# A down projection with seven block products in place of eight, and one load fewer of the packed half tile

## The chip, the cores and the metric

One core of one Trainium2 chip. The metric is the device time of one execution in microseconds: the kernel before takes 1940.79 us (median of 3 runs, 1940.75 to 1940.89). Besides, one execution was recorded by the hardware profiler. The engines are TensorE (PE; its weight loads are PEld), VectorE (DVE), ScalarE (ACT), GpSimd (POOL) and SyncE (SP), which only issues DMAs here.

## The reference, cut to what matters

```python
# x: 16 rows of 128 tokens, 1024 features, after a state-space layer and attention
def _qlinear(x, q, scale, A, Bm):          # q: integers 0..15
    w = (q.astype(jnp.float32) - 7.5) * (scale * 0.005)[:, None]
    y = jnp.einsum('bsh,oh->bso', x, w)
    return y + 0.02 * (x @ A @ Bm)
g = _qlinear(x, gate_q, gate_scale, gate_A, gate_B)    # 1024 -> 2752
u = _qlinear(x, up_q, up_scale, up_A, up_B)            # 1024 -> 2752
h = jax.nn.silu(g) * u
out = x0 + _qlinear(h, down_q, down_scale, down_A, down_B)   # 2752 -> 1024
```

A matrix product is computed with the levels (q - 7.5) as exact 16-bit numbers and the other operand split into a high and a low 16-bit part, so each block product is two matmuls. The scale is applied behind it.

## The kernel before, in words

The program has four stages: the state-space layer (to some 210 us), attention (to some 950 us), the gate and up projections (to 1629 us) and the down projection (to the end).

**Gate and up.** There are 44 jobs; a job is one tile of 128 hidden features for one half of the tokens (`JOBS`). Jobs 0 and 1 are computed whole, jobs 2 and 3 are the last, half-filled tile (64 gate rows and 64 up rows packed into one), once for each half of the tokens, and from job 4 on (`SEVENS`) each job takes seven block products for eight. For each job SP loads the integer levels into the one buffer `qraw` (`load_rows`), ACT turns them into 16-bit levels (`convert`, one of two buffers `q16`), POOL forms the sums of level blocks that the seven products need (`level_sums`), PE multiplies, and DVE and ACT form the hidden values, whose low part DVE (jobs 0 to 3) or POOL (`low_hidden`) makes, and SP stores them to DRAM. From job 23 on (`SECOND`) SP also loads the levels of the down projection, one of 22 tiles in each job and two in three of them (`TWICE`), into one buffer; POOL converts each one job later (`convert_levels`). SP's loads wait in the program's order: `load_rows` for the conversion that frees `qraw`, `load_levels` for POOL's conversion of the tile before.

**Down.** There are 16 row tiles of 128 tokens. For a tile, `down` runs over the 22 tiles of hidden features (21 full ones with a high and a low part, one with the packed half), with the 1024 outputs as two halves of 512: 86 matmuls of 512 columns into `acc`. In their middle `low_term` (2 matmuls) computes the low-rank part; ACT scales it into `lrt` (`down_term`), POOL adds the residual, DVE scales the sums (`y`) and adds `lrt`, and SP stores. Three buffers `parts` hold the hidden values of a tile, 1376 KB each. The last tile is computed one half after the other, so that little is left behind its last matmul.

## Time and profile before

| what | value |
|---|---|
| median of 3 runs | 1940.79 us |
| the profiled execution's own time | 1940.61 us |
| its span, first to last instruction | 1938.8 us |
| PE busy | 1813.0 us, 94% |
| DVE busy | 1201.4 us, 62% |
| ACT busy | 714.1 us, 37% |
| POOL busy | 860.2 us, 44% |
| mean granted TensorE clock | 0.989 |

The busy share of an engine is an average over four stages with different limits. The granted clock is given as a share of 2.4 GHz. In the views a duration is from an instruction's start to its end, and pipelined instructions overlap a little, so that a step from one start to the next may be shorter than the duration.

### The profile page before, as it was taken

The numbers are of one execution on the slowest core, as the hardware profiler recorded it, in microseconds if no ns is written. First come the engines' busy times: TensorE is split into PE (matmuls) and PEld (weight loads), VectorE is DVE, ScalarE is ACT, GpSimd is POOL, SyncE is SP. The second block draws the span as 40 slices with busy tenths as digits, with TensorE's granted clock in tenths as the row PEclk, the third lists the DMA queues.
The fourth block names the chain that finished last, engine by engine and source line by source line (L and its number), as shares of the span: only waits on it lengthen the run. The fifth ranks groups of instructions, "written<-read, shape, count | busy, mean of one in ns | idle before, by whom it ended". The sixth has DMA issues, their size and how long they took to land.

```text
span 1938.8 us, 31415 instructions
## 1 busy us (share of the span) xinstructions
PE 1813.0 (94%) x12892; PEld 990.2 (51%) x12892; DVE 1201.4 (62%) x1570; ACT 714.1 (37%) x1027; POOL 860.2 (44%) x593
## 2 busy tenths in 40 slices
PE   0586999999999999999999899999999999999999
PEld 0586665656666656545554344444444444444444
DVE  8996577787878888855657677775755554111111
ACT  4478243343433344422114454453544443000000
POOL 6973134343333334432361576665677774010111
PEclk9988999999999999999999899999999999999999
DMA  2122211111112211144531333434455544434341
GB/s 97 44 66 67 62 56 22 34 39 41 52 53 78 80 60 61 66 158 167 165 104 55 120 109 120 130 99 141 142 181 177 171 155 153 153 102 153 107 148 44
DMA packets 102847, 195.44 MB, mean 101 GB/s; under 512 B 14320, under 2 KB 75504, under 8 KB 92208
## 3 DMA queue, kind: packets, MB, share of 16 engines
q1 hardware_dynamic: 102704, 193.43, 31.2%
q8 instruction: 103, 1.69, 0.4%
q14 instruction: 40, 0.33, 0.1%
HBM read 136.24 MB, written 56.11 MB: 99 GB/s over the span
## 4 chain that ended last, share of the span: by engine, by line
PE 75%; DVE 9%; POOL 2%; issue 2%; ACT 2%; DMA 1%; DVEq 0%; SPq 0%; ACTq 0%
PE acc L1511 15%; PE acc L1377 12%; PE acc L1379 12%; PE ps_p L1169 4%; PE ps_p L1171 4%; PE ps_p L1170 4%; PE acc L1283 3%; PE acc L1285 3%; PE acc L1284 3%; PE ps_t L1196 3%; PE ps_p L1185 2%; PE ps_p L1186 2%; PE ps_p L1187 2%; PE ps_l L1386 2%; POOL prob L1058 1%
## 5 line engine op out<-in xcount | busy, mean ns | idle before, releaser
L1058 POOL TENSOR_TENSOR prob<-prob,mx 128x1024 f32<-128x1024 f32 x64 | 121.4, 1896 | 371.0 <-DVE mx L1878 371.0
L1169 PE MATMUL ps_p<-x_hi,w_qk 128*128 128x512 f16 x512 | 194.7, 380 | 0.0
L1170 PE MATMUL ps_p<-x_lo,w_qk 128*128 128x512 f16 x512 | 194.0, 379 | 0.0
L1171 PE MATMUL ps_p<-x_hi,w_qk 128*128 128x512 f16 x512 | 194.0, 379 | 0.0
L2265 DVE TENSOR_TENSOR y<-acc,down_scale 128x1024 f32<-128x1024 f32 (+1 forms) x17 | 19.8, 1162 | 252.8 <-PE acc L1511 252.8
L1111 POOL TENSOR_TENSOR hidden<-up,hidden 128x512 f16<-128x512 f32 x80 | 91.1, 1160 | 143.0 <-ACT hidden L1737 142.8
L1159 POOL TENSOR_TENSOR lr_term<-lr_term,h_again 128x1024 f32<-128x1024 f32 x16 | 37.6, 2348 | 253.6 <-ACT lr_term L1825 253.6
L1185 PE MATMUL ps_p<-w_v,x_hi 128*128 128x256 f16 x512 | 140.7, 275 | 3.7 <-PEq L805 3.6
L1063 POOL TENSOR_TENSOR prob<-prob,sm 128x1024 f32<-128x1024 f32 x64 | 120.1, 1896 | 52.9 <-DVE sm L1885 52.9
L1186 PE MATMUL ps_p<-w_v,x_hi 128*128 128x256 f16 x512 | 140.7, 275 | 0.0
L1187 PE MATMUL ps_p<-w_v,x_lo 128*128 128x256 f16 x512 | 140.6, 275 | 0.0
L1571 ACT ACTIVATE pth<-ps_t 128x512 f16<-128x512 f32 x128 | 76.1, 595 | 163.8 <-PE ps_t L1196 163.7
L258 PE MATMUL ssm_ps<-phase,magnitude 128*128 128x128 f32 x512 | 70.7, 298 | 64.9 <-DVE magnitude L469 61.7
L2130 DVE SCALAR_TENSOR_TENSOR up<-acc,gu_scale,up 128x512 f32<-128x512 f32 x120 | 90.0, 750 | 61.1 <-PE acc L1379 60.0
L2130 DVE SCALAR_TENSOR_TENSOR gate<-acc,gu_scale,gate 128x512 f32<-128x512 f32 x120 | 89.7, 748 | 56.1 <-PE acc L1379 55.3
L1377 PE MATMUL acc<-x_hi,q_f 128*128 128x512 f16 x320 | 122.3, 382 | 0.0
L1379 PE MATMUL acc<-x_lo,q_f 128*128 128x512 f16 x320 | 122.2, 382 | 0.0
L1377 PE MATMUL acc<-x_hi,q_sums 128*128 128x512 f16 x320 | 121.7, 380 | 0.0
L1379 PE MATMUL acc<-x_lo,q_sums 128*128 128x512 f16 x320 | 121.3, 379 | 0.0
L1377 PE MATMUL acc<-x_sum,q_sums 128*128 128x512 f16 x320 | 121.3, 379 | 0.0
L1379 PE MATMUL acc<-x_sum,q_sums 128*128 128x512 f16 x320 | 121.3, 379 | 0.0
L1889 DVE SCALAR_TENSOR_TENSOR ptl<-ps_t,pth 128x512 f16<-128x512 f32 x128 | 87.7, 685 | 47.2 <-ACT pth L1571 46.8
(343 smaller groups left out, 4382.6 us busy)
## 6 DMA issues: line engine op xcount, KB each, us to landing
q_raw<-in_gu_q SPq DMA_DIRECT2D x42, 1024.0 KB, 6.2
hid_parts<-hidden_parts SPq DMA_DIRECT2D x16, 1376.0 KB, 6.6
hidden_parts<-hidden SPq DMA_DIRECT2D x42, 512.0 KB, 3.5
down_raw<-in_down_q SPq DMA_DIRECT2D x22, 512.0 KB, 3.7
w_raw<-in_w_qk SPq DMA_DIRECT2D x8, 1024.0 KB, 4.9
h_tokens<-n_tok SPq DMA_DIRECT2D x16, 512.0 KB, 3.7
o_parts<-ot SPq DMA_DIRECT2D x32, 256.0 KB, 2.3
wv_raw<-in_w_o SPq DMA_DIRECT2D x8, 1024.0 KB, 4.8
```

Source lines behind the costliest of these rows:

```text
L1058: nc.gpsimd.tensor_tensor(prob[s % 2][p][:], prob[s % 2][p][:], bc(mx[p][:], H, 2), ALU.subtract).then_inc(s_sub[p], 1)
L1063: nc.gpsimd.tensor_tensor(prob[s % 2][p][:], prob[s % 2][p][:], bc(sm[p][:], H, 2), ALU.mult).then_inc(s_prob[p], 1)
L1169: nc.tensor.matmul(out[:], w[:, j % 2, m, 0, at], xn_hi[:, k, tok], start=(k == 0), stop=False)
L1170: nc.tensor.matmul(out[:], w[:, j % 2, m, 0, at], xn_lo[:, k, tok], start=False, stop=False)
L1171: last = nc.tensor.matmul(out[:], w[:, j % 2, m, 1, at], xn_hi[:, k, tok], start=False, stop=(k == KT - 1))
L1185: nc.tensor.matmul(out, xn_hi[:, k, tok], wv[:, g % 2, 0, at], start=(k == 0), stop=False)
L1186: nc.tensor.matmul(out, xn_hi[:, k, tok], wv[:, g % 2, 1, at], start=False, stop=False)
L1187: last = nc.tensor.matmul(out, xn_lo[:, k, tok], wv[:, g % 2, 0, at], start=False, stop=(k == KT - 1))
L1377: nc.tensor.matmul(banks[bank], lev[:, k * P:(k + 1) * P], hi[:, k, :], start=(k == 0 and not adds), stop=False, skip_group_check=adds)
L1379: last = nc.tensor.matmul(banks[bank], lev[:, k * P:(k + 1) * P], lo[:, k, :], start=False, stop=(k == KH - 1), skip_group_check=adds)
L1511: last = nc.tensor.matmul(acc[n % 2][:, b, :], parts[n % 3][:, at], levels[i][:, b * CH:(b + 1) * CH], start=(i == 0 and part == 0), stop= ...
L2130: stt(to[:], banks[bank], scl[:, m, i:i + 1], to[:], ALU.mult, ALU.add).then_inc(s_read, 1)
```

## The change

**The down projection.** Tiles 0 and 1 stay as they are. The other 14 tiles form seven pairs (`q` from 1). For a pair, the first 20 of the 22 tiles of hidden features are cut in two blocks of 10 (`KD`), the outputs in two halves, and the two row tiles are the two rows of a 2 by 2 block product. It is made with seven block products of 20 matmuls in place of eight, by Winograd's form of Strassen's scheme. The last two tiles of hidden features are added in the old way (3 matmuls for each row tile and half). The products, in PE's order, are p1, p6, p5, p2, p22 (only the rest of one quarter), p7, p3 and p4.

Four of the products take sums of hidden values, and four take sums of level blocks. The sums of levels are made once: sum 3 by POOL (`level_sum(3, i)`, 10 instructions), sums 1, 2 and 4 by DVE (30). The sums of hidden values are made for every pair, in two pieces of 640 columns: sum 1 (`f1`) and sum 3 (`f3`) by POOL in float32, in three steps each (`hid_one`, `hid_three`), sums 2 (`f2`) and 4 (in `f1` again) by DVE in two steps each; ACT copies each to a 16-bit high part (`high_hid_sum`) and DVE subtracts for the low part (`low_hid_sum`). `one_and_two` is what DVE does for sums 1 and 2, `three_and_four` for sums 3 and 4. p6 takes sum 2, p5 sum 1, p7 sum 3, p3 sum 4.

The product p1 is wanted in three quarters: ACT copies it out of PSUM (`first_down`), and DVE adds the products from PSUM one after the other (`sum_down`: v, x5, x22, x7, c12, c21). `parts` has four buffers, loaded two by two. The hidden values are scaled by a power of two that is four times smaller, so that the sums fit.

**The half tile.** Jobs 2 and 3 use the same levels. They are now loaded and converted once (`LOADS` gives the number of a job's load), and the loads behind come one job earlier in SP's order; the conversion for job 4 takes the place of that for job 3 in ACT's.

The diff, cut:

```diff
+KD = 10
+DP = C // 2
+DOWN_PROD = ("p1", "p6", "p5", "p2", "p22", "p7", "p3", "p4")
+DOWN_READ = ("v", "x5", "c11", "x22", "x7", "c12", "c21")
 NJ = len(JOBS)
+LOADS = [g if g < SEVENS - 1 else g - 1 for g in range(NJ)]
...
+    parts = [put(f"hid_parts{k}", [P, HB], F16, room) for k, room in enumerate(("ot", "w", "v1", "v0"))]
...
+    f1 = put("hid_f1", [P, KD // 2, P], F32, "probt", 5120)
...
+            sp.wait_ge(s_q, LOADS[g])
...
-            if 0 < g < NJ - 2:
-                load_rows(g + 2)
+            if g < 2:
+                load_rows(g + SEVENS)
+            if 2 < g < NJ - 3:
+                load_rows(g + 3)
...
+        def residual_and_term(n):
             pool.wait_ge(s_h1d[n % 2], 16 * (n // 2 + 1))
             pool.wait_ge(s_lrt, n + 1)
...
+            tt(lrt[n % 2][:], lrt[n % 2][:], h1d[n % 2][:], ALU.add).then_inc(s_sum, 1)
+        def hid_one(q, h):
+            n = 2 * (q - 1) + h
+            pool.wait_ge(s_parts[(2 * q + 1) % 4], 16 * ((2 * q + 1) // 4 + 1))
+            if h:
+                pool.wait_ge(s_dl[0], n)
+                pool.wait_ge(s_f2, n)
+            elif q > 1:
+                pool.wait_ge(s_dl[3], n)
+            chain.after(tt(f1[:], hid_piece(2 * q + 1, 0, h, 0), hid_piece(2 * q + 1, 1, h, 0), ALU.add))
+            chain.after(tt(f1[:], f1[:], hid_piece(2 * q + 1, 0, h, 1), ALU.add))
+            tt(f1[:], f1[:], hid_piece(2 * q + 1, 1, h, 1), ALU.add).then_inc(s_f1, 1)
+        def hid_three(q, h):
+            pool.wait_ge(s_parts[2 * q % 4], 16 * (2 * q // 4 + 1))
+            if q > 1:
+                pool.wait_ge(s_dl[2], 2 * (q - 2) + h + 1)
+            to = f3[h]
+            chain.after(tt(to[:], hid_piece(2 * q, 0, h, 0), hid_piece(2 * q + 1, 0, h, 0), ALU.subtract))
+            chain.after(tt(to[:], to[:], hid_piece(2 * q, 0, h, 1), ALU.add))
+            tt(to[:], to[:], hid_piece(2 * q + 1, 0, h, 1), ALU.subtract).then_inc(s_f3, 1)
+        pool.wait_ge(s_prod, PROD.total)
+        for i in range(KD):
+            tt(level_sum(3, i), level_block(1, 1, i), level_block(0, 1, i), ALU.subtract).then_inc(s_l3, 1)
+        for q in range(DP):
+            if q + 1 < DP:
+                hid_one(q + 1, 0)
+            residual_and_term(2 * q)
+            if q + 1 < DP:
+                hid_three(q + 1, 0)
+                hid_three(q + 1, 1)
+                hid_one(q + 1, 1)
+            residual_and_term(2 * q + 1)
...
+        def down_block(bank, of_hid, of_levels, adds, ends):
+            for i in range(KD):
+                for part in two:
+                    last = nc.tensor.matmul(banks[bank], of_hid(i, part), of_levels(i), start=(not adds and i == 0 and part == 0),
+                                            stop=(ends and i == KD - 1 and part == 1), skip_group_check=adds)
+            return last
...
+        for q in range(1, DP):
+            n, m = 2 * q, 2 * q + 1
+            pe.wait_ge(s_parts[n % 4], 16 * (n // 4 + 1))
+            if q == 1:
+                pe.wait_ge(s_y1, 1)
+            else:
+                pe.wait_ge(s_dread, dread(q - 1, "c11"))
+            down_block(0, lambda i, part: hid_part(n, i, part), lambda i: level_block(0, 0, i), False, True).then_inc(s_dprod, 1)
+            pe.wait_ge(s_dl[1], 2 * q)
+            if q == 1:
+                pe.wait_ge(s_l2, KD)
+            else:
+                pe.wait_ge(s_dread, dread(q - 1, "c21"))
+            down_block(1, lambda i, part: dsum[1][part][:, i, :], lambda i: level_sum(2, i), False, True).then_inc(s_dprod, 1)
+            pe.wait_ge(s_dl[0], 2 * q)
+            if q == 1:
+                pe.wait_ge(s_l1, KD)
+                pe.wait_ge(s_y1, 2)
+            else:
+                pe.wait_ge(s_dread, dread(q - 1, "c12"))
+            down_block(2, lambda i, part: dsum[0][part][:, i, :], lambda i: level_sum(1, i), False, True).then_inc(s_dprod, 1)
             low_term(n)
...
+            pe.wait_ge(s_dfirst, q)
+            down_block(0, lambda i, part: hid_part(n, KD + i, part), lambda i: level_block(1, 0, i), True, False)
+            down_rest(0, n, 0, True).then_inc(s_dprod, 1)
+            pe.wait_ge(s_parts[m % 4], 16 * (m // 4 + 1))
+            if q > 1:
+                pe.wait_ge(s_dread, dread(q - 1, "x22"))
+            down_rest(3, m, 1, False).then_inc(s_dprod, 1)
+            pe.wait_ge(s_dl[2], 2 * q)
+            if q == 1:
+                pe.wait_ge(s_l3, KD)
+            pe.wait_ge(s_dread, dread(q, "v"))
+            down_block(1, lambda i, part: dsum[2][part][:, i, :], lambda i: level_sum(3, i), True, True).then_inc(s_dprod, 1)
+            pe.wait_ge(s_dl[3], 2 * q)
+            pe.wait_ge(s_dread, dread(q, "x5"))
+            down_block(2, lambda i, part: dsum[3][part][:, i, :], lambda i: level_block(1, 1, i), True, False)
+            down_rest(2, n, 1, True).then_inc(s_dprod, 1)
+            low_term(m)
+            if q == 1:
+                pe.wait_ge(s_l4, KD)
+            pe.wait_ge(s_dread, dread(q, "x7"))
+            down_block(1, lambda i, part: hid_part(m, KD + i, part), lambda i: level_sum(4, i), True, False)
+            down_rest(1, m, 0, True).then_inc(s_dprod, 1)
...
-            if 2 <= g + 1 <= SEVENS:
-                convert(g + 1)
+            if g == 1:
+                convert(2)
+            if g == 2:
+                convert(SEVENS)
...
-            if SEVENS < g + 1 < NJ:
+            if SEVENS <= g < NJ - 1:
...
+        def high_hid_sum(q, k, h, src, made):
+            act.wait_ge(made, 2 * (q - 1) + h + 1)
+            if q > 1:
+                act.wait_ge(s_dprod, dprod(q - 1, ("p5", "p6", "p7", "p3")[k]))
+            nc.scalar.activation(piece(dsum[k][0], h), src[:], ACT.Copy).then_inc(s_dh[k], 1)
+        def first_down(q):
+            act.wait_ge(s_dprod, dprod(q, "p1"))
+            if q > 1:
+                act.wait_ge(s_dread, dread(q - 1, "c21"))
+            nc.scalar.activation(first_d[:], acc[0][:, 0, :], ACT.Copy).then_inc(s_dfirst, 1)
+        act.wait_ge(s_prod, PROD.total)
+        for q in range(DP):
+            if q:
+                for h in two:
+                    high_hid_sum(q, 2, h, f3[h], s_f3)
+                    high_hid_sum(q, 3, h, f1, s_f4)
+                first_down(q)
+            down_term(2 * q)
+            if q + 1 < DP:
+                for h in two:
+                    high_hid_sum(q + 1, 0, h, f1, s_f1)
+                    high_hid_sum(q + 1, 1, h, f2[h], s_f2)
+            down_term(2 * q + 1)
...
+        def low_hid_sum(q, k, h, src):
+            dve.wait_ge(s_dh[k], 2 * (q - 1) + h + 1)
+            tt(piece(dsum[k][1], h), src[:], piece(dsum[k][0], h), ALU.subtract).then_inc(s_dl[k], 1)
+        def one_and_two(q, h):
+            to = f2[h]
+            low_hid_sum(q, 0, h, f1)
+            dve.wait_ge(s_parts[2 * q % 4], 16 * (2 * q // 4 + 1))
+            chain.after(tt(to[:], f1[:], hid_piece(2 * q, 0, h, 0), ALU.subtract))
+            tt(to[:], to[:], hid_piece(2 * q, 0, h, 1), ALU.subtract).then_inc(s_f2, 1)
+            low_hid_sum(q, 1, h, to)
+        def three_and_four(q, h):
+            low_hid_sum(q, 2, h, f3[h])
+            if h:
+                dve.wait_ge(s_dl[3], 2 * q - 1)
+            else:
+                dve.wait_ge(s_dl[0], 2 * q)
+            chain.after(tt(f1[:], hid_piece(2 * q, 1, h, 0), f2[h][:], ALU.subtract))
+            tt(f1[:], f1[:], hid_piece(2 * q, 1, h, 1), ALU.add).then_inc(s_f4, 1)
+            low_hid_sum(q, 3, h, f1)
+        def sum_down(q, name, product, bank, to, other, behind):
+            dve.wait_ge(s_dprod, dprod(q, product))
+            if behind:
+                dve.wait_ge(s_dread, dread(q, behind))
+            tt(to, banks[bank], other, ALU.add).then_inc(s_dread, 1)
...
+        def last_down(q):
+            sum_down(q, "c21", "p4", 1, y[1][:, left], first_d[:], None)
+            dve.wait_ge(s_dread, dread(q, "c21"))
+            scaled(y[1], left)
...
+        dve.wait_ge(s_prod, PROD.total)
+        for i in range(KD):
+            tt(level_sum(1, i), level_block(0, 1, i), level_block(0, 0, i), ALU.subtract).then_inc(s_l1, 1)
...
+        scale_sums(0)
+        one_and_two(1, 0)
+        one_and_two(1, 1)
+        dve.wait_ge(s_half, 1)
+        for i in range(KD):
+            dve.wait_ge(s_l3, i + 1)
+            tt(level_sum(2, i), level_sum(3, i), level_block(0, 0, i), ALU.add).then_inc(s_l2, 1)
+        for i in range(KD):
+            dve.wait_ge(s_l2, i + 1)
+            tt(level_sum(4, i), level_block(1, 0, i), level_sum(2, i), ALU.subtract).then_inc(s_l4, 1)
+        scale_sums(1)
+        for q in range(1, DP):
+            if q > 1:
+                last_down(q - 1)
+                add_term(2 * q - 1, slice(0, D))
+            for h in two:
+                three_and_four(q, h)
...
+            dve.wait_ge(s_dfirst, q)
+            sum_down(q, "v", "p6", 1, y[0][:, right], first_d[:], None)
+            dve.wait_ge(s_yout[1], 16 * q)
+            sum_down(q, "x5", "p5", 2, y[1][:, right], first_d[:], None)
+            dve.wait_ge(s_dprod, dprod(q, "p2"))
+            tt(y[0][:, left], banks[0], scl_d[:, left], ALU.mult).then_inc(s_dread, 1)
+            sum_down(q, "x22", "p22", 3, y[1][:, right], y[1][:, right], "x5")
+            if q + 1 < DP:
+                one_and_two(q + 1, 0)
+            sum_down(q, "x7", "p7", 1, y[1][:, right], y[1][:, right], "x22")
+            dve.wait_ge(s_dread, dread(q, "x7"))
+            scaled(y[1], right)
+            if q + 1 < DP:
+                one_and_two(q + 1, 1)
+            sum_down(q, "c12", "p3", 2, y[0][:, right], y[0][:, right], "v")
+            dve.wait_ge(s_dread, dread(q, "c12"))
+            scaled(y[0], right)
+            add_term(2 * q, slice(0, D))
+        add_term(C - 1, right)
+        last_down(DP - 1)
+        add_term(C - 1, left)
```

**POOL in the down projection.** Before, its rows are all alike, one for each row tile: the term plus the residual.

```order
L1159 TENSOR_TENSOR lr_term_2033<-lr_term_2033,h_again_2037 128x1024
L1159 TENSOR_TENSOR lr_term_2032<-lr_term_2032,h_again_2036 128x1024
L1159 TENSOR_TENSOR lr_term_2033<-lr_term_2033,h_again_2037 128x1024
L1159 TENSOR_TENSOR lr_term_2032<-lr_term_2032,h_again_2036 128x1024
L1159 TENSOR_TENSOR lr_term_2033<-lr_term_2033,h_again_2037 128x1024
```

Now, for one pair (`hid_f_2041` is the one buffer f1, `hid_f_2044` is f3 of the first piece, `hid_parts_2031` and `2032` are the two row tiles of the next pair); the three rows of L1241 to L1243 come once more for `hid_f_2045`, and the first three rows once more behind them:

```order
L1231 TENSOR_TENSOR hid_f_2041<-hid_parts_2032 128x640
L1232 TENSOR_TENSOR hid_f_2041<-hid_f_2041,hid_parts_2032 128x640
L1233 TENSOR_TENSOR hid_f_2041<-hid_f_2041,hid_parts_2032 128x640
L1220 TENSOR_TENSOR lr_term_2047<-lr_term_2047,h_again_2051 128x1024
L1241 TENSOR_TENSOR hid_f_2044<-hid_parts_2031,hid_parts_2032 128x640
L1242 TENSOR_TENSOR hid_f_2044<-hid_f_2044,hid_parts_2031 128x640
L1243 TENSOR_TENSOR hid_f_2044<-hid_f_2044,hid_parts_2032 128x640
```

POOL has twelve instructions more for a pair, nine of them between the two additions of the residual, and f1 is written by both of its groups and by DVE.

**DVE in the down projection.** Before, two rows for each row tile, the scaling and the sum:

```order
L2265 TENSOR_TENSOR y_2034<-acc,down_scale 128x1024
L2268 TENSOR_TENSOR y_2034<-y_2034,lr_term_2032 128x1024
L2265 TENSOR_TENSOR y_2035<-acc,down_scale 128x512
L2268 TENSOR_TENSOR y_2035<-y_2035,lr_term_2033 128x512
L2265 TENSOR_TENSOR y_2035<-acc,down_scale 128x512
L2268 TENSOR_TENSOR y_2035<-y_2035,lr_term_2033 128x512
```

Now, from x7 of one pair into the next: L2473 are the sums from PSUM (x7, c12, c21), L2478 the scaling, L2483 the sum with the term, L2446 to L2454 `one_and_two` for the next pair's second piece, and behind the last row here comes `three_and_four`.

```order
L2473 TENSOR_TENSOR y_2050<-acc,y_2050 128x512
L2478 TENSOR_TENSOR y_2050<-y_2050,down_scale 128x512
L2446 TENSOR_TENSOR hid_sum_2034<-hid_f_2041,hid_sum_2033 128x640
L2453 TENSOR_TENSOR hid_f_2043<-hid_f_2041,hid_parts_2029 128x640
L2454 TENSOR_TENSOR hid_f_2043<-hid_f_2043,hid_parts_2029 128x640
L2446 TENSOR_TENSOR hid_sum_2036<-hid_f_2043,hid_sum_2035 128x640
L2473 TENSOR_TENSOR y_2049<-acc,y_2049 128x512
L2478 TENSOR_TENSOR y_2049<-y_2049,down_scale 128x512
L2483 TENSOR_TENSOR y_2049<-y_2049,lr_term_2047 128x1024
L2473 TENSOR_TENSOR y_2050<-acc,first_down 128x512
L2478 TENSOR_TENSOR y_2050<-y_2050,down_scale 128x512
L2483 TENSOR_TENSOR y_2050<-y_2050,lr_term_2048 128x1024
```

The reads of PE's banks (c12, c21) stand behind the second `one_and_two`, which needs POOL's last f1 of the next pair.

**ACT at jobs 2 to 4.** Before, the conversion of job 4's levels (128x2048) stands behind job 2's hidden values and ahead of the four copies into `x_hi` (sum 2 of the tokens for job 4) and of job 3's terms:

```order
L1676 ACTIVATE q_f_1972<-q_raw,q_zero 128x1024
L1716 ACTIVATE first_gate<-ps_l,g_half_back 128x512
L1729 ACTIVATE gate_1959<-gate_1959 128x512
L1716 ACTIVATE first_up<-ps_l,g_half_back 128x512
L1729 ACTIVATE gate_1956<-gate_1956 64x512
L1676 ACTIVATE q_f_1971<-q_raw,q_zero 128x2048
L1744 ACTIVATE x_hi<-sum_2006 128x512
```

Now:

```order
L1827 ACTIVATE q_f_1972<-q_raw,q_zero 128x2048
L1867 ACTIVATE first_gate<-ps_l,g_half_back 128x512
L1880 ACTIVATE gate_1959<-gate_1959 128x512
L1867 ACTIVATE first_up<-ps_l,g_half_back 128x512
L1880 ACTIVATE gate_1956<-gate_1956 64x512
L1895 ACTIVATE x_hi<-sum_2006 128x512
```

Job 4's conversion has moved ahead of job 2's terms, where the (half as long) one of job 3 stood.

## Rows read from the trace of the kernel before

**Rows 1.** Busy time in stretches: busy us of each engine, clock, DMA share, GB/s

```profile
1070.00:1080.00 10.00, 3.71 (x18) 1.46 (x16) 1.52 (x2) 5.48 (x8) 4.34 (x4) 0.83 0.23 92
1080.00:1090.00 10.00, 7.40 (x25) 2.71 (x26) 9.67 (x14) 5.07 (x10) 0.67 (x1) 0.66 0.42 131
1630.00:1930.00 300.00, 300.00 (x1391) 137.14 (x1390) 41.31 (x37) 22.59 (x24) 39.84 (x18) 1.00 0.38 130
```

**Rows 2.** Chain that ended last, in the down projection: start, us, what

```profile
1629.07 6.91 PE acc L1511 x32
...
1659.17 18.58 PE acc L1511 x86
1677.74 0.46 PE ps_l L1523 x2
...
1921.02 13.84 PE acc L1511 x64
1934.89 0.70 DVE y L2265
```

**Rows 3.** Groups by line and shape from 1000 us: busy us, mean ns, idle before

```profile
L2130 DVE SCALAR_TENSOR_TENSOR up<-acc,gu_scale,up 128x512 f32<-128x512 f32 x120 | 90.0, 750 | 61.1 <-PE acc L1379 60.0 <-DVE up L2121 0.5
...
L1729 ACT ACTIVATE gate<-gate 128x512 f32<-128x512 f32 x84 | 52.6, 626 | 132.1 <-DVE gate L2130 132.1
...
L1159 POOL TENSOR_TENSOR lr_term<-lr_term,h_again 128x1024 f32<-128x1024 f32 x16 | 37.6, 2348 | 253.6 <-ACT lr_term L1825 253.6
...
L2268 DVE TENSOR_TENSOR y<-y,lr_term 128x1024 f32<-128x1024 f32 x15 | 18.4, 1225 | 0.5
...
L1825 ACT ACTIVATE lr_term<-ps_l,g_down_back 128x1024 f32<-128x1024 f32 x16 | 17.8, 1114 | 263.6 <-PE ps_l L1523 263.6
...
L1074 POOL TENSOR_TENSOR sum<-x_hi 128x512 f32<-128x512 f16 x4 | 4.6, 1154 | 0.0
...
L2268 DVE TENSOR_TENSOR y<-y,lr_term 128x512 f32<-128x512 f32 x2 | 1.4, 692 | 0.1
...
L2273 DVE TENSOR_SCALAR down_scale<-down_scale,g_down_scale 128x1024 f32<-128x1024 f32 x1 | 0.8, 755 | 1.2 <-DMA down_scale<-in_down_scale 1.2
```

**Rows 4.** Timeline of POOL, in one job: start, us, what, idle before

```profile
1111.38 1.60 POOL L1106 TENSOR_TENSOR q_sums<-q_f,q_sums 128x512 f16<-128x512 f16 x1
```

**Rows 5.** Timeline of DVE, in the same stretch

```profile
1100.03 2.99 DVE L2136 TENSOR_TENSOR up<-gate,up 128x512 f32<-128x512 f32 x2 [0.70 <-ACT gate L1729]
...
1110.33 1.64 DVE L2170 TENSOR_TENSOR sum<-sum,x_hi 128x512 f32<-128x512 f32 x1
...
1114.88 1.29 DVE L2136 TENSOR_TENSOR up<-gate,up 128x512 f32<-128x512 f32 x2
```

**Rows 6.** Timeline around jobs 3 and 4: SP, ACT and PE

```profile
1067.06 0.58 SPq L978 DMA_DIRECT2D q_raw<-in_gu_q  x1
...
1073.28 2.00 ACT L1676 ACTIVATE q_f<-q_raw,q_zero 128x2048 f16<-128x2048 int32 x1 [7.67 <-DMA q_raw<-in_gu_q]
...
1082.60 1.01 PE L1386 MATMUL ps_l<-low_stack,gu_b_stack 128*128 128x512 f16 x2 [8.88 <-ACT first_up L1716]
```

**Rows 7.** Timeline of POOL in the second pass

```profile
1500.68 1.15 POOL L1104 TENSOR_TENSOR q_sums<-q_sums,q_f 128x512 f16<-128x512 f16 x1
1501.91 1.16 POOL L1105 TENSOR_TENSOR q_sums<-q_f 128x512 f16<-128x512 f16 x1
...
1504.26 2.77 POOL L1115 TENSOR_SCALAR x_lo<-down_raw 128x1024 f16<-128x1024 int32 x1
1510.72 2.28 POOL L1111 TENSOR_TENSOR hidden<-up,hidden 128x512 f16<-128x512 f32 x2 [3.69 <-ACT hidden L1737]
```

**Rows 8.** DMA issues: KB each, median us from issue to landing

```profile
hid_parts<-hidden_parts SPq DMA_DIRECT2D x16, 1376.0 KB, 6.6
...
down_raw<-in_down_q SPq DMA_DIRECT2D x22, 512.0 KB, 3.7
...
down_b_raw<-in_down_b SPq DMA_DIRECT2D x1, 512.0 KB, 7.2
```

138 lines of the change are left out of this document (87 added, 51 removed).

## The prediction, on record before the changed kernel was run

> **What bounds the kernel now.** I read the busy time in stretches first. From 1630 to 1930 us TensorE is busy for 300.00 us of 300 at full clock, while DVE has 41, ACT 23 and POOL 40 us of work [rows 1]. The chain of waits says the same: from 1629.07 to 1934.86 (1921.02 + 13.84) it is matmuls, then 0.70 us of DVE; a row tile is 86 matmuls in 18.58 us, 0.216 each, and 0.47 for the low-rank term [rows 2]. A pair of tiles thus takes 38.1 us. The one gap of note is at job 4: TensorE waits 8.88 us until 1082.60, behind ACT, which waited 7.67 us for the load of job 4's levels; the load was issued only at 1067.06 [rows 6]. The granted clock then falls to 0.83 and 0.66 of 2.4 GHz in the two stretches of 10 us, that is, between the two levels [rows 1]. So both parts of the change aim at TensorE; whether they gain depends on what the other engines must now do between products.
>
> **TensorE's own saving.** A pair has 152 matmuls for 172: 20 x 0.216 = 4.3 us, so 33.8 us for 38.1. Seven pairs would save 30.2 us, if nothing came late.
>
> **What the sums cost.** All row-tile sums are 640 columns wide, a shape that the trace lacks, so I go along the line between 512 and 1024 columns [rows 3]. POOL: 1.154 and 2.348, so 1.45; a dependent instruction starts 0.08 behind the end of the one before (1500.68 to 1501.91 for 1.15) [rows 7], so 1.53. DVE: 0.692 and 1.225, so 0.83, with 0.04 between dependent ones 0.87. ACT: 0.626 for 512 in SBUF and 1.114 for 1024 from PSUM, so 0.75 at most; I take 0.73. A hand-over between engines is about 0.08 (from 0.03 to 0.14 in the timelines).
>
> By sheer busy time each engine fits in 33.8 us: POOL 12 x 1.53 + 2 x 2.4 = 23.2; DVE 16 x 0.87 for hidden sums, 7 + 3 of 512 columns at 0.73 and 2 of 1024 at 1.26, together 23.7; ACT 8 x 0.73 + 0.69 + 2 x 1.11 = 8.8. But they wait for each other in a ring, because the one buffer f1 carries sum 1 (POOL) and sum 4 (DVE), and DVE's program reads PSUM behind its second `one_and_two`. I follow the ring for one pair:
>
> - POOL can start f1 of the next pair only when `three_and_four` is over. It then runs f1 (3 instructions), the residual, f3 twice (6) and f1 again (3): 12 x 1.53 + 2.4 = 20.8.
> - ACT's copy, DVE's low part and two sums, ACT's copy, DVE's low part, with four hand-overs: 0.73 + 3 x 0.87 + 0.73 + 0.87 + 0.3 = 5.3.
> - c12, its scaling, the 1024-column sum, c21, its scaling, the 1024-column sum: 0.73 + 0.73 + 1.26 + 0.73 + 0.73 + 1.26 = 5.4.
> - `three_and_four` for both pieces: each 3 x 0.87, ACT's 0.73, 0.87 and two hand-overs, 4.37; twice 8.7, and 0.08 to POOL: 8.8.
>
> That is 40.3 us, more than the 33.8 of TensorE and than the 38.1 of before. In the ring TensorE isn't a member: p3 ends some 14 us before DVE reads it, and p4 some 5 us before. p1 of the next pair (4.3) hides a part of the wait; p6 waits some 10 us for sum 2 and for c21 to free its bank, p2 another 1.3 for `first_down`, which ACT's order holds behind the last copy of `three_and_four`.
>
> **Collisions.** DVE's instructions with both operands in SBUF and POOL's sums stretch each other: the same pair of L2136 takes 1.29 us alone and 2.99 beside POOL, L2170 takes 1.64, where a sum of this size alone takes 0.69 [rows 3, 5], and POOL's L1106 1.60 for 1.16 [rows 4, 7]; L2130, with one operand in PSUM, has a mean of 0.750 over 120 instructions, most of them in stretches in which POOL works too [rows 3]. The stretches fit a strict alternation. In the ring POOL's nine instructions from f3 on meet four 640-column ones of `one_and_two` and one scaling: 4 x 0.44 x 640/512 + 0.45 = 2.7. And the scaling behind c12 meets POOL's 2.35 of the second residual: +1.8. So 44.8 us a pair.
> The Trainium skill ("SBUF — State Buffer", section "Who interferes with whom") says that VectorE and GpSimd share one port pair as an exclusive lock, taken by a VectorE instruction with two SBUF inputs against a GpSimd one that reads SBUF, the loser standing still. By that rule the ring is 44.8 us, without it 40.3; the rows just read agree with the rule (2.99 for 1.29).
>
> **The first pair.** Counted from 1629.07. Tiles 0 and 1 end at 39.1. POOL has 10 level sums (until 15), waits for `parts` 3 (issued at 8, 6.6 later [rows 8]), and ends the second f1 at 41.4, with the residual, f3 and some collisions; DVE's `one_and_two` ends at 48. Then come 20 level sums on DVE ahead of the scaling of tile 1. For a level sum (512 columns, all 16-bit) there is no row: independent 512-column sums follow each other in 0.60 (0.69 less 0.09 of overlap); as the lower bound, L2273 shows DVE passing 1024 columns with one tensor operand in 0.755, which halved is 0.38, less overlap some 0.33. I take 0.60, the row of the same operation: 12 us, +2 beside the residual, 1.3 for the scaling and 1.3 for the sum, and `three_and_four` 8.7 with `first_down` 0.7: p2 starts at 74.6. p2, p22, p7, p3 and p4 are 92 matmuls and a term, 20.4, without waits of note: p4 ends at 95.0. At 0.33 all 30 level sums are 8.1 us less: 86.9.
>
> **The sum.** 95.0 + 6 x 44.8 = 363.8, against 305.8 before: +58.0. Tail: c21, scaling and sum (3 x 0.73) for DVE's two instructions of before: +0.8.
> The half tile: SP can issue job 4's load as soon as job 2's levels are converted, long before it is needed. ACT converts it in place of job 3's, 2.00 us for about half, and this 1.0 delays job 3, whose last product was over at 1082.60 - 8.88 = 1073.7 [rows 6]: now 1074.7, and behind ACT's term and the hand-over (0.7) TensorE starts job 4 at 1075.4, 7.2 us early. The 25 matmuls from 1080 to 1090 took 7.40 us at the low clock, at 0.216 apiece 5.4 [rows 1]: another 1.9. Together -9.1; from -4 (the hidden chain of DVE is late next, with POOL's level sums now beside it) to -11.
> Second pass: the loads of rows stand one job earlier in SP's order, ahead of that of a down level. Such a 512 KB load takes 3.7 us to land; the one of down_b, which SP issues right behind a load of rows, took 7.2 [rows 8]. In the job of the rows it would be issued at some 1500.2 and land at 1507.4, where POOL wanted it at 1504.26; with 2.77 it is over just before the next hidden part at 1510.72 [rows 7], so single loads cost nothing; the two double ones at jobs 29 and 35 make `level_sums` some 1.2 late each: +2.4 (0 to 6).
> Sum: +58.0 + 0.8 - 9.1 + 2.4 = +52.1 on the profiled execution's 1940.6, so 1992.7; the median lies 0.2 above that execution: 1993.
>
> **Rivals.**
> 1. *Level sums at the low bound* (8.1 less): 1985. The one-operand row speaks for it, the rows of two-operand sums against it. The Trainium skill ("VectorE: DVE Perf Modes", "The perf-mode tier table") gives `tensor_tensor` twice the rate where all tensors are 16-bit; by it the sum would be this one, and no row here shows it.
> 2. *The ring without collisions*, because the instructions pass each other: 40.3 a pair. With the first pair free of them too (85.0 where 95.0 stood): 85.0 + 6 x 40.3 = 326.8, so +21.0 + 0.8 - 9.1 + 2.4 = +15.1: 1956. The stretched pairs of L2136 speak against it.
> 3. *The other side: TensorE stays the bound*, since DVE, ACT and POOL each have under 24 us of work in 33.8. It needs the ring under 33.8, which is POOL's 640 columns at under some 0.9 us where 512 take 1.15. Then 39.1 + some 10 of waits in the first pair + 7 x 33.8 = 285.7: -20.1 + 0.8 - 9.1 + 2.4 = -26.0: 1915. It decides from a ring of 38.1 - 1 on.
> 4. *The half tile's load gives nothing*: the wait passes to DVE's sums of job 3 and the 9.1 go: 2002.
> 5. *The clock*: after the 10 us wait before p6 one must expect the low clock for a while, as behind the wait that ended at 1082.60 (0.66 in that stretch [rows 1], some 1.9 us of work late). The slack between p6 and p2 and that behind p4 (5 us) take this up. Only if it stayed at half for most of a pair (152 x 2 x 0.216 = 66 us) would TensorE be the bound again; six such pairs would add 120 us. I hold it for unlikely, since the clock is 1.00 again in the long stretch [rows 1] and the matmuls in between had come down to 0.30 on average.
>
> **How the numbers follow.** Forecast (ring of 44.8, level sums at 0.60) 0.39; rival 1 0.33; rival 2 0.11; rival 3 0.09; rival 4 0.05; rival 5 0.03. A difference of under 0.2% (3.9 us) is what can't be told from none; a case between rivals 2 and 3 would have to fall there. Faster 0.09, same 0.02, slower 0.89. The forecast's own range, with POOL's step at 1.4 to 1.6 for 1.53 (12 x 0.1 = 1.2 a pair, 8 in all) and the bounds of the two small terms, is 1982 to 2006. For 8 in 10 with rival 1 and some of rival 2: 1955 to 2008.
>
> **What would show it right or wrong.** In the profile after, the period from p4 to p4 should be about 44.8 us with TensorE busy for 33.8; DVE's c12 should start right behind its second `one_and_two` of the next pair and not behind p3; POOL's first instruction of a pair should be released by DVE's low part of sum 4, and its group of f3 instructions should average near 2 us against 1.45 for the second f1. TensorE's waits should stand before p6 (DVE) and p2 (ACT). At job 4 the 8.88 us should be under 2. A period of 40 us says that collisions were priced too high; one near 34, with TensorE without waits, that the ring isn't one and the forecast is wrong in its sign.

## The result and the profile after

The changed kernel is slower: 1988.11 us (median of 4 runs, 1985.11 to 1990.57) against 1940.77 for the kernel before; the ratio is 1.0245, with a 95% interval of 1.0227 to 1.0263. Its profiled execution took 1988.77 us with a span of 1986.9. The forecast of 1993 is 0.2% off and its sign right, but that it is so close is in part luck, since two of its terms were wrong in opposite directions: the down projection came out 24.9 us shorter than forecast, and the second pass 15.3 us longer.

The answer to [rows 1] first: busy time in stretches of the kernel after (busy us and count for PE, PEld, DVE, ACT and POOL, clock, DMA share, GB/s). The last stretch is one pair of tiles.

```profile
1070.00:1080.00 10.00, 9.13 (x37) 3.39 (x36) 7.25 (x10) 4.67 (x9) 1.18 (x1) 0.83 0.17 52
1080.00:1090.00 10.00, 9.78 (x46) 4.13 (x44) 9.14 (x15) 5.67 (x8) 1.38 (x2) 1.00 0.20 35
1643.00:1943.00 300.00, 259.40 (x1135) 114.65 (x1134) 187.67 (x208) 57.67 (x79) 177.65 (x109) 0.93 0.33 122
1792.99:1834.82 41.83, 35.85 (x159) 16.00 (x158) 26.81 (x29) 8.27 (x11) 23.61 (x15) 0.92 0.33 119
```

TensorE, busy for all 300 us before, is now busy for 259 of 300. The down stage begins at 1643.2 (before: 1629.07, [rows 2]) and its last product ends at 1982.1: 338.9 us for 305.8, so +33.1. The other +14.1 lie ahead of it.

The chain of waits answers [rows 2]. In that stage it was matmuls from end to end; now, over this pair of tiles, there is not one in it (start, us, what; the short pieces called issue are left out):

```profile
1792.99 1.41 POOL hid_f L1231
...
1797.31 2.37 POOL lr_term L1220
1799.67 1.37 POOL hid_f L1241
...
1801.11 1.86 POOL hid_f L1242
...
1813.49 1.41 POOL hid_f L1233
1814.92 0.74 ACT hid_sum L1988
...
1815.69 0.83 DVE hid_sum L2446
...
1819.65 0.69 DVE y L2473
1820.37 2.55 DVE y L2478
1822.95 1.23 DVE y L2483
1824.17 0.61 DVE y L2473
1824.81 0.70 DVE y L2478
...
1826.76 0.74 DVE hid_sum L2446
...
1833.85 0.84 DVE hid_sum L2446
...
1834.82 1.41 POOL hid_f L1231
```

It goes through POOL's sums of the next pair (L1231 is the first of f1), ACT's copy and DVE's second `one_and_two`, then without a wait c12 (1819.65), its scaling (2.55 us, beside POOL's residual addition, where the scaling of c21 takes 0.70), c21, and `three_and_four`, whose last low part releases the next f1 41.83 us after the first. POOL's timeline gives the same release:

```profile
1834.82 1.40 POOL L1231 TENSOR_TENSOR hid_f<-hid_parts 128x640 f32<-128x640 f16 x1 [12.45 <-DVE hid_sum L2446]
```

TensorE's waits in the stage are (us in total, times, longest). The first row is the wait before p6, once in each pair but the first:

```profile
PE acc L1634 <- DVE y L2473: 35.2, 6, 6.4
PE acc L1634 <- DVE x_lo L2505: 8.7, 1, 8.7
PE acc L1634 <- ACT first_down L1994: 2.6, 1, 2.6
```

Some of the groups that answer to [rows 3] (us busy, mean ns): POOL's residual addition, DVE's scaling, two of POOL's three f3 instructions, one of its f1, and one of DVE's for sum 4. The mean of L1241, the first instruction of each f3, is 1688 ns.

```profile
L1220 POOL TENSOR_TENSOR lr_term<-lr_term,h_again 128x1024 f32<-128x1024 f32 x16 | 38.6, 2413 | 63.8 <-ACT lr_term L1978 63.8
L2478 DVE TENSOR_TENSOR y<-y,down_scale 128x512 f32<-128x512 f32 x21 | 28.5, 1358 | 0.7
L1242 POOL TENSOR_TENSOR hid_f<-hid_f,hid_parts 128x640 f32<-128x640 f32 x14 | 26.1, 1867 | 1.1
L1243 POOL TENSOR_TENSOR hid_f<-hid_f,hid_parts 128x640 f32<-128x640 f32 x14 | 25.4, 1814 | 1.1
L1232 POOL TENSOR_TENSOR hid_f<-hid_f,hid_parts 128x640 f32<-128x640 f32 x14 | 19.6, 1399 | 1.1
L2465 DVE TENSOR_TENSOR hid_f<-hid_f,hid_parts 128x640 f32<-128x640 f32 x14 | 11.5, 825 | 0.5
```

**Ahead of the down stage.** At job 4 TensorE's wait of 8.88 us [rows 6] has become 0.87, but the wait ahead of job 3's second bank is 3.36, where it was 1.55 (the first row is of before, the others of after):

```profile
1065.44 0.38 PE L1370 MATMUL acc<-x_hi,q_f 128*128 128x512 f16 x1 [1.55 <-DVE up L2113]
...
1068.96 0.38 PE L1467 MATMUL acc<-x_hi,q_f 128*128 128x512 f16 x1 [3.36 <-DVE up L2291]
1079.80 0.59 PE L1483 MATMUL ps_l<-low_stack,gu_b_stack 128*128 128x512 f16 x2 [0.87 <-ACT first_up L1867]
```

By job 5 the kernel after is 4.07 us ahead of the one before; it was 1.7 behind at 1050 already, where the kernels don't differ, so 5.8 come from the half tile. It stays 4.07 ahead until job 31. Then it loses 9.46 us between the starts of jobs 31 and 32 and 8.24 between those of jobs 37 and 38, behind the two double level loads (SP's turns 29 and 35) with loads of rows around them: 17.7 in all. In job 31 it waits 6.6 us in two times:

```profile
1452.28 0.89 PE L1501 MATMUL ps_i<-hidden,down_a 128*64 128x512 f16 x4 [2.04 <-POOL hidden L1172]
1457.75 0.61 PE L1474 MATMUL acc<-x_hi,q_sums 128*128 128x512 f16 x1 [4.57 <-POOL q_sums L1167]
```

The other 2.9 of the 9.46 are slower matmuls: the granted clock is 0.50 (1.2 of 2.4 GHz) from 1457.75 to 1461.75 and back at 1.00 by 1465.80. In job 37 the waits are 1.9 and 4.8, and 1.5 is the clock.

Here is SP's queue at the first of them, after and then before, and POOL's conversion in both:

```profile
1440.89 0.33 SPq L1022 DMA_DIRECT2D q_raw<-in_gu_q  x1
1441.27 8.97 SPq L1035 DMA_DIRECT2D down_raw<-in_down_q  x2
...
1452.26 0.38 SPq L1067 DMA_DIRECT2D hidden_parts<-hidden  x1
```

```profile
1431.37 0.38 SPq L1021 DMA_DIRECT2D hidden_parts<-hidden  x1
1431.79 0.58 SPq L978 DMA_DIRECT2D q_raw<-in_gu_q  x1
1439.02 6.89 SPq L991 DMA_DIRECT2D down_raw<-in_down_q  x2
```

```profile
1447.12 2.77 POOL L1176 TENSOR_SCALAR x_hi<-down_raw 128x1024 f16<-128x1024 int32 x1 [9.67 <-DMA down_raw<-in_down_q]
1449.97 2.26 POOL L1172 TENSOR_TENSOR hidden<-up,hidden 128x512 f16<-128x512 f32 x2
1452.18 1.15 POOL L1164 TENSOR_TENSOR q_sums<-q_f 128x512 f16<-128x512 f16 x1
```

```profile
1442.78 2.77 POOL L1115 TENSOR_SCALAR x_hi<-down_raw 128x1024 f16<-128x1024 int32 x1 [3.79 <-DMA down_raw<-in_down_q]
1445.63 2.27 POOL L1111 TENSOR_TENSOR hidden<-up,hidden 128x512 f16<-128x512 f32 x2
1447.86 1.16 POOL L1103 TENSOR_TENSOR q_sums<-q_f 128x512 f16<-128x512 f16 x1
```

Shifted by the 4.07 us, the level should have been asked for at 1434.95 and converted at 1438.71. It is asked for at 1441.27, 6.3 late, since SP now first waits for ACT's conversion of job 31, and takes 5.85 to land for 3.76, since 1 MB of rows is in front of it. POOL's conversion, hidden part and level sums are all 8.4 late, because in a double turn POOL converts the very level that SP issues in that turn; in a single turn it converts the one of the turn before, and the delay is hidden, as forecast. The medians from issue to landing on the profile's page say the same, against 3.7 and 6.6 of [rows 8]:

```profile
hid_parts<-hidden_parts SPq DMA_DIRECT2D x16, 1376.0 KB, 8.8
...
down_raw<-in_down_q SPq DMA_DIRECT2D x22, 512.0 KB, 6.6
```

### The profile page after: what moved, and what is told of

The parts are those of the page before. It is cut to its first block, busy times and chain, and to the rows that moved or that the text cites. A ratio compares the mean times of both kernels' runs of the same rounds, so it can differ in the third digit from the quotient of the medians.

```text
span 1986.9 us, 31616 instructions
## 1 busy us (share of the span) xinstructions
PE 1803.8 (91%) x12752; PEld 980.2 (49%) x12752; DVE 1375.4 (69%) x1767; ACT 755.3 (38%) x1089; POOL 1009.2 (51%) x687
## 4 chain that ended last, share of the span: by engine, by line
PE 55%; DVE 14%; POOL 11%; issue 4%; ACT 3%; DMA 2%; POOLq 0%; SPq 0%; DVEq 0%; ACTq 0%
PE acc L1474 10%; PE acc L1476 10%; PE ps_p L1266 4%; PE ps_p L1268 3%; PE ps_p L1267 3%; PE acc L1380 3%; PE acc L1381 3%; PE acc L1382 3%; PE ps_t L1293 3%; PE ps_p L1282 2%; PE ps_p L1284 2%; PE ps_p L1283 2%; PE ps_l L1483 1%; POOL hid_f L1242 1%; POOL hid_f L1243 1%
## 5 line engine op out<-in xcount | busy, mean ns | idle before, releaser
L1634 PE MATMUL acc<-x_hi,hid_sum 128*128 128x512 f16 x336 | 89.8, 428 | 43.9 <-DVE y L2473 35.2
L1988 ACT ACTIVATE hid_sum<-hid_f 128x640 f16<-128x640 f32 x56 | 40.4, 733 | 233.1 <-DVE hid_f L2465 82.7
```

## The experiments

Twelve kernels; all times as medians, the ratios against the kernel before run on the same chip. "Period" is the time from POOL's first f1 of a pair to that of the next, as the mean of the last four such steps.

| kernel | us | ratio (95%) | period |
|---|---|---|---|
| after | 1988.1 | 1.0245 (1.0227 to 1.0263) | 42.0 |
| e1_load_alone | 1953.9 | 1.0073 (1.0061 to 1.0085) | |
| e2_load_behind_store | 1934.3 | 0.9969 (0.9957 to 0.9981) | |
| e3_after_behind_store | 1970.5 | 1.0158 (1.0145 to 1.0171) | 42.0 |
| e4_sums_alone | 1974.9 | 1.0183 (1.0170 to 1.0196) | 41.9 |
| e5_sum4_in_f3 | 1965.3 | 1.0124 (1.0104 to 1.0144) | 40.9 |
| e6_row_sums_first | 1958.8 | 1.0094 (1.0080 to 1.0108) | 40.7 |
| e7_all_three | 1951.7 | 1.0054 (1.0042 to 1.0067) | 39.3 |
| e8_p1_half | 1968.9 | 1.0145 (1.0130 to 1.0161) | 41.9 |
| e9_f3_two_steps | 1949.3 | 1.0040 (1.0027 to 1.0054) | 39.0 |
| e10_orders | 1945.0 | 1.0023 (1.0014 to 1.0033) | 38.5 |
| e11_scale_in_psum | 1936.4 | 0.9978 (0.9970 to 0.9987) | 37.4 |
| e12_residual_earlier | 1928.2 | 0.9937 (0.9925 to 0.9949) | 35.8 |

### The load of the half tile and the second pass

**e1_load_alone**: the kernel before with the edits of `LOADS` alone.

```
-            if 0 < g < NJ - 2:
-                load_rows(g + 2)
+            if g < 2:
+                load_rows(g + SEVENS)
+            if 2 < g < NJ - 3:
+                load_rows(g + 3)
```

> The kernel before with the one load of the half tile alone (its SP order included: rows of job g + 3 asked for ahead of the down level), the down projection as before. Theory A, read from the profile after: the half tile gives 5.8 us back (TensorE's start of job 5 against that of before, less the shift that was there already), and the two double level loads cost 9.5 and 8.2 us, since the first level of the pair now lands behind a 512 KB load of rows and POOL stands at its conversion with the level sums behind it: 1940.8 - 5.8 + 17.7 = 1952.7. Rival B: the 17.7 belong to the new down stage (its buffers and semaphores), and the load alone gives its 5.8: 1935.0. Rival C, the prediction's own term: +2.4 for the two double loads: 1937.4.

Measured: 1.0073, which is +14.2 us (11.8 to 16.5), with TensorE waiting for q_sums at the same two places. Theory A (+11.9) holds, at the lower end of the interval; B (-5.8) and the prediction's own term (-3.4) are excluded. (The load of rows in front of the level is 1 MB, not 512 KB as the expectation has it.)

**e2_load_behind_store**: from job 23 on, the rows are asked for last in SP's turn.

```
+            if 2 < g < SECOND and g < NJ - 3:
+                load_rows(g + 3)
...
             sp.dma_start(dst, src).then_inc(s_out[g % 2], 16)
+            if SECOND <= g < NJ - 3:
+                load_rows(g + 3)
```

> As e1_load_alone, but from job 23 on the load of rows is issued at the end of SP's turn, behind the store, so that the down level goes first again. Theory A: the 17.7 go and the 5.8 stay: 1935.0 (1932 to 1937), with TensorE's waits for q_sums at the double loads gone. Rival B: the same 1935 as for e1_load_alone. Rival D: the level lands late because the rows of a job later are in flight at all, wherever they are issued: some of the 17.7 stay, 1940 to 1953.

Measured: 0.9969, -6.0 us (-8.3 to -3.7): theory A (-5.8). From 1400 to 1650 us the trace has no wait of TensorE left. The load is worth some 6 us, and its place in one queue costs some 20.

**e3_after_behind_store**: the same move in the kernel after.

> The kernel after with that one move in SP's turn (rows behind the store from job 23 on). Theory A: 1988.1 - 17.7 = 1970.4. Rival B: no change, 1988. The down stage must keep its 338.9 us and its period of 41.8 us a pair.

Measured: 1970.5 us, 1.0158 for 1.0245, so 16.9 us less by the ratios and 17.6 by the medians, as theory A had it; the period stays at 42.0.

**e4_sums_alone**: the kernel after with `LOADS[g]` replaced by `g` and the old loads and conversions.

> The block products of the down projection alone, with the half tile loaded twice and SP's order as before. Theory A: the down stage takes 338.9 us for 305.8, and nothing else changes: 1940.8 + 33.1 = 1973.9. Rival B (the second pass is slowed by what comes with the new down stage): 1973.9 + 17.7 = 1991.6.

Measured: 1974.9 us, +35.5 us (33.0 to 38.1) by the ratio; theory A had +33.1. So the two parts of the change add up (14.2 + 35.5 = 49.7, for 47.3 together), and neither gains as it was made. All kernels below are built on e3.

### What the ring of the down stage is made of

**e8_p1_half**: `down_block` of p1 runs over 5 of its 10 tiles, so this kernel leaves out half of the product.

> e3_after_behind_store, leaving out half of product p1 (10 of its 20 matmuls) in each of the seven pairs, so TensorE has 2.2 us less in each. Theory A (TensorE is no member of the ring): the period stays at 41.8, only the first pair may gain: 1968 to 1971. Rival B (TensorE sets the pace): 7 x 2.2 = 15 less, 1955.

Measured: 1968.9 us, 2.5 less by the ratios (1.0145 for 1.0158, the intervals overlap), period 41.9; TensorE's work is 15 us less (70 matmuls) and only its waits before p6 grow, from 34.7 us in e3 to 50.1. TensorE is not in the ring.

**e9_f3_two_steps**: one POOL instruction fewer in each f3; this kernel leaves out the low part of the second row tile in sum 3.

```
-            chain.after(tt(to[:], to[:], hid_piece(2 * q, 0, h, 1), ALU.add))
-            tt(to[:], to[:], hid_piece(2 * q + 1, 0, h, 1), ALU.subtract).then_inc(s_f3, 1)
+            tt(to[:], to[:], hid_piece(2 * q, 0, h, 1), ALU.add).then_inc(s_f3, 1)
```

> e3_after_behind_store, leaving out POOL's third instruction of each f3 (the part subtracted last), so 14 POOL instructions fewer, two in each pair. Theory A (POOL's sums are members of the ring): each is 1.69 us by its group's mean plus 0.08 between dependent ones, 3.5 a pair, so the period falls from 41.8 to 38.3 and the time to 1970.5 - 6 x 3.5 = 1949.5 (1947 to 1956, since a part of the collisions may move to the instructions that are left). Rival: POOL isn't in the ring, 1970.

Measured: 1949.3 us, 21.2 less than e3, for the 21 expected; the period is 39.0, 3.0 less for 3.5, and the first pair gives the rest. POOL's sums are in the ring, though POOL is busy for only 56% of e3's steady stretch (94.7 of 167.8 us).

**e5_sum4_in_f3**: the buffer that should close the ring is taken out of it (`to` is `f3[h]`; the copy, the low part and POOL's waits follow).

```
-            chain.after(tt(f1[:], hid_piece(2 * q, 1, h, 0), f2[h][:], ALU.subtract))
-            tt(f1[:], f1[:], hid_piece(2 * q, 1, h, 1), ALU.add).then_inc(s_f4, 1)
+            chain.after(tt(to[:], hid_piece(2 * q, 1, h, 0), f2[h][:], ALU.subtract))
+            tt(to[:], to[:], hid_piece(2 * q, 1, h, 1), ALU.add).then_inc(s_f4, 1)
```

> e3_after_behind_store with sum 4 written over sum 3 in f3 and not into f1, so that POOL can begin f1 of the next pair without waiting for three_and_four. Theory A (the period of 41.8 us is the ring through POOL's sums, one_and_two, DVE's row-tile sums and three_and_four): POOL's first f1 (4.4) and the residual (2.4) leave the path between three_and_four and f3, so at most 6.8 us a pair, less what they now cost three_and_four in collisions, 2 to 4: period 37 to 39.5, and 1970.5 - 6 x 2.3 to 4.8 = 1942 to 1957. Rival B (DVE by its own work and the collisions is the bound): the period stays at 41.8 and the time at 1970.

Measured: 1965.3 us, period 40.9: a miss. The wait for the buffer went (from 79.0 us to 0.8), but POOL's first f1 now waits 61.4 us in six times, up to 11.6, for the load of `parts`, which SP asks for only behind p4 and the residual of the pair before. Only 1.1 of 6.8 us a pair are left. So the run shows that the wait at f1 can be moved, but what f1 alone costs it does not show.

**e6_row_sums_first**: c12, its scaling and `add_term(2 * q)` stand ahead of `one_and_two(q + 1, 1)`.

> e3_after_behind_store with c12, its scaling and the sum with the term moved ahead of DVE's second one_and_two of the next pair. Theory A: these three (0.7 + 2.5 + 1.3 = 4.5 us) are done while DVE waits for POOL's second f1 and leave the ring; some 2 of it may come back as collisions with POOL's sums: period 37.3 to 39.5, so 1970.5 - 14 to 27 = 1943 to 1957. Rival B (DVE's work is the bound, the order of it doesn't matter): 1970. Rival C (POOL is the bound, with its 12 sums and 2 residuals back to back): no change, 1970.

Measured: 1958.8 us, period 40.7, 1.2 less; both just outside the range. Part of the 4.5 us comes back, as DVE now does these instructions while POOL's f3 and second f1 run.

**e7_all_three**: e5 and e6, and `hid_one(q + 1, 1)` ahead of `hid_three(q + 1, 1)`.

> e5 and e6 together, and POOL's second f1 ahead of its second f3. Theory A: no ring is left that is longer than TensorE's 33.8 us by steps alone (POOL 12 x 1.48 + 4.8 = 22.6, DVE some 23); what is left above it are the collisions. The period comes to 35 to 38, and the time to 1970.5 - 6 x 3.8 to 6.8 = 1930 to 1948. If TensorE is the bound again (33.8), 1922. If the shared SBUF access of DVE and POOL is the bound, their instructions with both operands in SBUF alternate strictly: POOL's 22.6 and DVE's 16 of 640 columns at 0.8, 3 of 512 at 0.7 and 2 of 1024 at 1.2, 17.3, make 39.9, and the time is 1959.

Measured: 1951.7 us, period 39.3: above theory A's range (35 to 38) and below strict alternation (39.9). Two waits of hand-overs were left, p2 behind `first_down` and f1 behind its load, which the next kernel takes away.

**e10_orders**: e7 with three orders changed.

```
                 high_hid_sum(q, 2, 0, f3[0], s_f3)
+                first_down(q)
                 high_hid_sum(q, 3, 0, f3[0], s_f4)
...
             store_rows(2 * q)
+            if q + 2 < DP:
+                ...
+                load_parts(2 * q + 5)
+                load_parts(2 * q + 4)
             next_residual(2 * q + 1)
...
         one_and_two(1, 0)
-        one_and_two(1, 1)
...
+        one_and_two(1, 1)
         scale_sums(1)
```

> e7_all_three with three more moves: ACT's first_down behind its first copy of sum 3 and not behind all four; SP's loads of the next rows ahead of its wait for the residual addition; DVE's level sums 2 and 4 ahead of the second one_and_two of the first pair. Theory A (what e7 still lacks are two waits in a row of hand-overs, p2 behind first_down with 20.9 us in all, and POOL's f1 behind the load, 44 us in all, 7.3 a pair, of which SP's late issue is some 4): 2 to 4 us less in each of six pairs and 5 to 6 in the first: 1951.7 - 5.5 - 12 to 24 = 1922 to 1934. Rival B (DVE and POOL alternate on SBUF, a pair costs 39.3 to 39.9 whatever the order): only the first pair gains, 1945 to 1947.

Measured: 1945.0 us, period 38.5. Both waits are gone from the trace, and yet almost nothing came of it beyond the first pair. In the traces the first pair is 6.5 us shorter than in e7 and the other six together 2.6: rival B, though its 39.3 to 39.9 a pair were 1 too high. The stretch of one pair shows why:

```profile
1781.10:1819.60 38.50, 35.16 (x156) 15.62 (x154) 34.91 (x29) 8.09 (x11) 27.74 (x16) 0.96 0.36 129
```

DVE is busy for 34.9 of 38.5 us. A pair's 28 instructions (the 29th is cut by the edge) at their undisturbed durations are 16 x 0.825 + 7 x 0.685 + 3 x 0.69 + 2 x 1.225 = 22.5 us. The other 12 are stretches beside POOL.

**e11_scale_in_psum**: the scales are copied into two idle banks of PSUM, and the scalings read them there.

```
-            chain.mark(tt(to[:, cols], to[:, cols], scl_d[:, cols], ALU.mult))
+            chain.mark(tt(to[:, cols], ps_i[1 if cols is right else 0][:], to[:, cols], ALU.mult))
```

> e10_orders with a copy of the scales (1024 columns) in two PSUM banks that are free in this stage, read by DVE's three scalings of each pair in place of the copy in SBUF, so that they have one operand in PSUM. The output is the same. Theory A (in e10 DVE is busy for 34.9 of 38.5 us of a pair, of which some 12 are stretches of instructions with both operands in SBUF beside POOL; such an instruction pays for POOL's access, one with an operand in PSUM doesn't): the scalings fall from a mean of 1.68 us to 0.69, 3.0 us less for DVE in each pair, of which a half may come back elsewhere: 1945.0 - 6 x 1.5 to 3 = 1927 to 1936. Rival B (DVE's instructions are long beside POOL wherever their operands lie, or the ring of hand-overs is what counts): the scalings stay near 1.7 us, and the time at 1945 to 1947 with the two copies.

Measured: 1936.4 us, period 37.4. The group of the scalings from 1700 to 1900 us, in e10 and then in e11:

```profile
L2477 DVE TENSOR_TENSOR y<-y,down_scale 128x512 f32<-128x512 f32 x17 | 26.8, 1577 | 0.6
```

```profile
L2477 DVE TENSOR_TENSOR y<-ps_i,y 128x512 f32<-128x512 f32 x17 | 11.8, 692 | 0.6
```

The same operation on as many columns takes 0.692 us for 1.577, by the place of one operand alone, and DVE's busy time of a pair falls from 34.9 to 30.3 of 37.4. So the stretch is a matter of two operands in SBUF beside POOL, and with it the time falls by 8.6 us. This is theory A, at its upper end (1936).

**e12_residual_earlier**: e11 with ACT's `down_term(2 * q)` ahead of `high_hid_sum(q, 3, 1, ...)`, and POOL's `hid_three(q + 1, 0)` ahead of `residual_and_term(2 * q)` and `hid_one(q + 1, 1)` behind both f3.

> e11_scale_in_psum with ACT's term of tile 2q ahead of its last copy of sum 4, and on POOL the first f3 of the next pair ahead of the residual addition. In e10 POOL stands 7.5 us a pair before that residual, behind ACT's term. Theory A, if hand-overs matter beside DVE's work: 0.5 to 1.5 us less a pair than e11, that is 3 to 9 less in all. If DVE's busy time alone is the bound: within 2 us of e11. Both kernels are worth running for their own time: at a pair under 36.9 us the block products would be faster than the kernel before with its half tile's load mended (1934).

Measured: 1928.2 us, period 35.8 (mean of four; single pairs 34.3 to 36.9), 8.2 less than e11. One pair of it:

```profile
1785.08:1821.51 36.43, 34.32 (x159) 15.50 (x157) 31.45 (x29) 8.27 (x11) 25.98 (x15) 1.00 0.38 136
```

TensorE is busy for 34.3 of 36.4 us at full clock. Hand-overs do matter beside the collisions: the period fell by 1.6 us, a little more than theory A's 0.5 to 1.5. In the trace the first pair is 4.3 us longer than in e11 and the other six together 12.1 shorter; which of the moves does which was not run. This version beats the kernel before (0.9937), and e2 too, the old down projection with the half tile's load mended (0.9969; the intervals don't meet).

## Why the prediction was right, and where it was wrong

**The ring held.** By the forecast's own segments, from the rows of the pair at 1792.99 to 1834.82:

| segment | forecast | measured |
|---|---|---|
| POOL's twelve sums and the residual | 20.8 + 2.7 | 21.9 (1792.99 to 1814.92) |
| second `one_and_two` | 5.3 | 4.7 (to 1819.65) |
| c12 to the last sum with a term | 5.4 + 1.8 | 7.1 (to 1826.76) |
| `three_and_four` | 8.8 | 8.1 (to 1834.82) |
| period | 44.8 | 41.8 |

The signs named in advance are there: f1 released by DVE's low part of sum 4, c12 right behind `one_and_two`, f3 at a mean of 1.69 to 1.87 us against 1.40 for f1, TensorE waiting before p6 (DVE). That TensorE is no member of the ring and POOL's sums are was shown by e8 and e9. That the buffer f1 closes it is read from the trace, where DVE's last low part of sum 4 releases POOL; e5 took that wait away, but another took its place. Of the 3.0 us too many in this pair, POOL gave half: a dependent step is 1.48 us for 1.53 and an independent one 1.36, and the 2.3 us of collisions there stand for 2.7. Two forecasts failed in small: p2 waited for `first_down` once only (2.6 us), where 1.3 a pair had been named, and p6 waited 5.9 us in the mean for some 10. TensorE is idle for 6.0 us of the pair where the forecast leaves 11.0 (44.8 - 33.8): 3 of the difference are the shorter period, and 2 the low clock behind each wait, as TensorE is busy for 35.9 us of the pair and not 33.8. That is rival 5's clock (0.67 from 1783 to 1789, behind the wait, and 1.00 from 1789), and as forecast the slack took it up. Rival 2 (no collisions, 40.3) had the nearer period, but for the wrong reason: its steps were too long, and with the steps as measured the period without collisions is 41.8 - 2.3 - 1.85 = 37.7.

**The first pair was forecast 7.4 us too long.** Its p4 ends 87.6 us after the stage's start, for 95.0. The term that was mis-sized is the level sum, taken at 0.60 us. In a row they take 0.34 each where POOL is idle (DVE's rows are of the chain, POOL's is of its timeline):

```profile
1689.81 4.91 DVE x_hi L2505 x8
...
1695.65 3.09 DVE x_lo L2508 x9
1698.74 1.15 DVE y L2439
```

```profile
1690.18 2.58 POOL L1220 TENSOR_TENSOR lr_term<-lr_term,h_again 128x1024 f32<-128x1024 f32 x1 [5.13 <-ACT lr_term L1978]
```

Here 9 take 3.09 (0.34 each). The 8 ahead of them take 4.91, because one of them, beside POOL's residual addition, takes 2.56 by itself, the "+2" of the forecast. The bound of 0.33 that was taken from a one-operand row was the right size. The Trainium skill's "VectorE: DVE Perf Modes" (section "The perf-mode tier table") has a `tensor_tensor` with all tensors of 16 bits run at twice the rate, and this row agrees. So rival 1 was right on the size, but its 8.1 us count 30 level sums: the ten of sum 1 are over at 1661.8 and DVE then waits, so only 20 are on the path, some 5.3.

Step by step, from the stage's start: the second `one_and_two` ends at 46.7 for 48; the 20 level sums with the residual beside them take 8.9 for 14; scaling and sum 2.4 for 2.6; from there to p2 it is 7.7 for 9.4. (The forecast's own steps add up to 74.0, not to its 74.6.) So p2 starts at 65.6, 9.0 early. Then p2 to p4 take 22.1 for 20.4, since p2 begins at the low clock behind TensorE's waits, which the forecast left out here: the same 12 matmuls take 4.32 us, and 2.77 in the later pair.

```profile
1708.73 4.32 PE L1634 MATMUL acc<-x_lo,hid_parts 128*128 128x512 f16 x12 [2.61 <-ACT first_down L1994]
...
1794.11 2.77 PE L1634 MATMUL acc<-x_lo,hid_parts 128*128 128x512 f16 x12
```

**The second pass failed.** The forecast said that the two double loads make `level_sums` some 1.2 us late each, +2.4, with an upper bound of 6. They cost 17.7, and e1 to e3 show that the place of `load_rows` in SP's turn is the whole cause. The step priced only the longer landing (7.2 for 3.7, which was about right: 6.6 in the median). It left out that SP, in program order, would first stand at ACT's conversion, 6.3 us, that the second conversion of a double turn stands ahead of the hidden part in POOL's order, and that TensorE's matmuls are slower behind each wait (4.3 of the 17.7). The split between SP's wait and the landing (6.3 and 2.1 of 8.4) is read from the trace; no run separates them. The forecast's claim that single loads cost nothing was right.

**The half tile** gave 5.8 us for 9.1 (e2: 6.0, with 3.7 to 8.3). The wait at job 4 went as forecast, but the one in job 3 grew from 1.55 to 3.36 us. Half of this is ACT's conversion ahead of job 2's terms (1.99 us for 1.13), which was forecast; the other half is that POOL's level sums now run beside DVE's two products there (2.25 us for 1.30), which the forecast had only as the reason of its lower bound, -4. It left out what follows: behind the longer wait the granted clock is 0.67 from 1068.96 to 1074.19, and the same matmuls take 1.7 us more. So job 3 is 3.5 late for 1.0, and job 4 starts 4.5 us early for 7.2.

**The sum.** -24.9 in the down stage (6 x 2.9 and 7.4), +15.3 in the second pass, +3.3 for the half tile, and +1.7 that was there ahead of all edits, -4.6 together; the profiled executions differ by 48.2 us for the 52.1 forecast. Of the 0.7 that are left, 0.6 are lost in job 43, where TensorE waits 0.54 us for q_sums. The total was closer than its terms, and that is luck: e3, which differs from the kernel after only by where SP asks for the rows from job 23 on, takes the second pass's loss away and lies at 1970.5, outside the forecast's own range of 1982 to 2006. Its reasoning on the sign of the down projection stands by e4; its size was too high by 24.9 of 58.0.

**The collisions** were priced at 4.5 a pair and came to 4.15. The rule of the Trainium skill's "SBUF — State Buffer" (section "Who interferes with whom") has VectorE instructions with two SBUF inputs and GpSimd instructions that read SBUF exclude each other; the scaling beside the residual (2.54 for 0.69) and above all e11 agree with it. What the forecast did not see is that the collisions would become the next bound once the ring was cut: I had counted DVE's 23.7 us and POOL's 23.2 us against TensorE's 33.8 one by one, but where both operands lie in SBUF the two hardly run side by side, and e10 is at 38.5. A strict alternation would be too high, though: it gives 22.6 + 17.3 = 39.9 for e10 (the sum of e7's expectation), and without the three scalings 37.8 for e11 and e12, which measured 37.4 and 35.8. It is an estimate from undisturbed durations, no lower limit.

## What to carry to other kernels

Before trading matmuls for elementwise sums, follow one turn of the sums through every buffer that two engines share and add up the steps and hand-overs; an engine that is busy for little over half of the period can still set it. As a first estimate add DVE's work with both operands in SBUF to POOL's rather than laying them side by side (here it was 0.4 to 2.0 us a pair too high); moving one operand of DVE's scalings to an idle PSUM bank took them out of that sum. When a load is moved ahead in a queue, look at what its own wait now holds back, not only at how long it takes to land. And price a wait of TensorE with the slower matmuls behind it.

## What the runs showed of the hardware

- A DVE multiplication of 512 columns in f32 took 1.577 us in the mean beside POOL with both operands in SBUF and 0.692 with one in PSUM (e10 and e11), the same as undisturbed.
- A DVE sum of 512 columns with all tensors in 16 bits follows the next at 0.34 us while POOL is idle, for 0.61 in f32 (1055.02 to 1055.63 in the kernel before). Beside POOL's level sums the steps are 1.1 to 1.3 us (1655.70 to 1659.40 in the kernel after), and beside its residual addition one took 2.56. POOL's own take 1.16 with f16 and with f32 inputs.
- POOL's sums of 640 columns took 1.40 us with f16 and f32 operands alike (L1231 and L1232), and DVE's 0.82; beside each other they took up to 1.98 and 2.02 (1804.87 and 1801.63 in the kernel after).
- The granted clock was 0.92 over a pair in which TensorE waited 6 us once, and 1.00 in e12's pair, where it waited 2.1 us in two times. In the down stage of the kernel after this cost nothing, as TensorE wasn't the bound; at the waits of the second pass it cost 4.3 us of 17.7.
